# One mLSTM + ternary FFN layer: keys and queries stacked per head by DMA through memory, or by VectorE copies

## What is computed

```python
x = x + attn(layernorm(x))      # mLSTM with 8 heads, 32 query/key and 64 value channels a head
x = x + ffn(layernorm(x))       # 512 -> 2048 -> 512, ternary weights, exact gelu
# attn: q, k, v, o = x @ Wq.T, x @ Wk.T, x @ Wv.T, x @ Wog.T; i, f = soft_cap(x @ W.T + b)
#  per step: C = F*C + I*k v^T; n = F*n + I*k; h = (q.C)/max(|q.n|, exp(-m)); norm over the head;
#  y = (sigmoid(o) * norm(h) * gamma) @ Wout.T
```

## Time and profile before

| | |
|---|---|
| Median of 3 runs | 2092.59 us (2092.44 to 2092.97) |
| The profiled execution | 2091.54 us |
| Its span, first to last instruction | 2089.8 us |
| TensorE busy | 1901.8 us, 91% of the span |
| VectorE busy | 1565.6 us, 75% |
| ScalarE, GpSimd busy | 1032.0 and 568.6 us |
| Mean granted TensorE clock | 0.957 of full speed |

### The profile page before, as it was taken

One profiled execution on the slowest core, in us unless ns is written; L12 is line 12 of the kernel. 1 busy time (PEld: TensorE's weight loads), 2 busy tenths in 40 slices (PEclk: granted clock), 3 DMA queues, 4 the chain that ended last, 5 costly groups with the idle time before them and its releaser, 6 DMA issues.

```text
span 2089.8 us, 26265 instructions
## 1 busy us (share of the span) xinstructions
PE 1901.8 (91%) x9652; PEld 1001.9 (48%) x9652; DVE 1565.6 (75%) x2798; ACT 1032.0 (49%) x1711; POOL 568.6 (27%) x401
## 2 busy tenths in 40 slices
PE   4667898998989899898989989898998989899989
PEld 2253454644545464454536445453644545364544
DVE  3887869687786968778696877869687796957742
ACT  3654627465362645536264553626455362645523
POOL 1242142240324224032422403232140323214030
PEclk7868999999999999999999999999999999999999
DMA  6232314142231404224140322414042241404010
GB/s 247 89 106 78 82 46 124 26 99 46 83 88 46 124 21 104 46 73 97 46 124 21 104 46 63 107 46 124 21 104 46 53 117 41 109 21 109 1 46 21
DMA packets 233504, 156.62 MB, mean 75 GB/s; under 512 B 195088, under 2 KB 199312, under 8 KB 228256
## 3 DMA queue, kind: packets, MB, share of 16 engines
q1 hardware_dynamic: 231792, 151.79, 27.5%
q10 hardware_dynamic: 1584, 3.15, 0.4%
HBM read 90.48 MB, written 17.24 MB: 52 GB/s over the span
## 4 chain that ended last, share of the span: by engine, by line
PE 63%; DVE 25%; issue 6%; ACT 5%; DMA 1%; POOL 0%; SPq 0%; POOLq 0%; DVEq 0%; ACTq 0%
PE pf L1687 21%; PE pf L1673 16%; PE pa L1574 11%; DVE hoT L1194 10%; DVE gT L1194 5%; PE ph L1646 4%; PE pa L1565 4%; DVE cst L1187 2%; PE ph L1640 2%; DVE gT L1124 2%; PE ph L1612 1%; DVE cst L1185 1%; PE ps L1623 1%; PE pa L1556 1%; ACT L768 1%
## 5 line engine op out<-in xcount | busy, mean ns | idle before, releaser
L1687 PE MATMUL pf<-w2T,gT 128*128 128x512 f16 x2048 | 535.2, 379 | 0.0
L1673 PE MATMUL pf<-x2T,w1T 128*128 128x512 f16 x2048 | 496.5, 396 | 0.9 <-DVE x2T L1320 0.6
L1574 PE MATMUL pa<-wT,xT 128*128 128x512 f16 x1536 | 344.7, 381 | 5.8 <-ACT vaug L788 2.9
L1673 PEld LDWEIGHTS pf<-x2T,w1T 128*128 128x128 f16 x2048 | 204.1, 102 | 236.5 <-issue 38.6
L574 POOL TENSOR_TENSOR hinv<-hvar,half 128x8 f32<-128x8 f32 x64 | 105.1, 1643 | 749.1 <-DVE hvar L1279 749.1
L1687 PEld LDWEIGHTS pf<-w2T,gT 128*128 128x128 f16 x2048 | 224.3, 111 | 173.9
L856 ACT ACTIVATE g<-pf,b1c 128x512 f32<-128x512 f32 x256 | 175.4, 685 | 237.6 <-DVE gT L1328 133.5
L1328 DVE SCALAR_TENSOR_TENSOR gT<-g,wscale,gT 128x512 f16<-128x512 f32 x256 | 190.9, 751 | 127.7 <-ACT gT L859 127.2
L1194 DVE COPY hoT<-cst 32x1024 f16<-32x1024 f16 x256 | 253.8, 991 | 4.6
L1574 PEld LDWEIGHTS pa<-wT,xT 128*128 128x128 f16 x1536 | 145.8, 98 | 193.1 <-ACT sig L795 14.0
L560 POOL TENSOR_TENSOR dec<-dec,causal 128x1024 f32<-128x1024 f32 x64 | 159.9, 2527 | 252.5 <-DMA dec<-gate_r 252.5
(11 more groups left out here) (202 smaller groups left out, 2407.3 us busy)
## 6 DMA issues: line engine op xcount, KB each, us to landing
dec<-gate_r SPq DMA_DIRECT2D x32, 1024.0 KB, 6.3
xin<-L_attn_x SPq DMA_DIRECT2D x16, 1024.0 KB, 5.9
out<-x1b SPq DMA_DIRECT2D x64, 256.0 KB, 2.3
xres<-L_attn_x SPq DMA_DIRECT2D x16, 512.0 KB, 6.3
xres<-L_attn_x SPq DMA_DIRECT2D x32, 256.0 KB, 3.0
qw<-gate_w SPq DMA_DIRECT2D x128, 48.0 KB, 5.7
gT<-L_ffn_w SPq DMA_DIRECT2D x5, 1024.0 KB, 4.9
gT<-L_ffn_w ACTq DMA_DIRECT2D x3, 1024.0 KB, 5.5
```

Of the source, the lines that this page charges most:

```text
L1574: last = nc.tensor.matmul(bank, src[:, xs, k, :], wT[:, ws, k, col:col + D], start=(k == 0 and n == 0), stop=(k == KD - 1 and n == 2))
L1673: last = nc.tensor.matmul(bank, w1T[:, k, tok(f)], x2T[:, part, :, k, :], start=(k == 0 and part == HI), stop=(k == KD - 1 and part == LO))
L1687: last = nc.tensor.matmul(bank, gT[:, part, f, tok(t)], w2T[:, f, :], start=(f == 0 and part == HI), stop=(f == NF - 1 and part == LO), sk ...
```

## The change

`stack_heads` and its 32 copies are gone. VectorE splits the keys, then waits until the split is stored, splits the queries into the same buffer, and goes on. SyncE's queue stores each split (0.5 MB) to a new tensor in memory, `kq_halves`, waits for the landing, and reads it back in four transfers of 32 partitions (256 KB each) straight into the stacked layout. The keys' store is issued before the transposition to `x2T`, everything else behind it. The heads now lie in `kst` and `qst` in the order in which the scores take them. TensorE waits once, before `scores(b, 0)`, for all eight read-backs. The `qw` loads become four transfers of 96 KB in place of eight of 48 KB.

```diff
--- before.py
+++ after.py
@@ -61,7 +61,7 @@
 
 
 
-DVE_L, DVE_A = 3, 6 + 4 + 4 * 5 + 4 + 2
+DVE_L, DVE_A = 3, 6 + 2 + 4 * 5 + 4 + 2
 POOL_A = 4
 
 
@@ -109,6 +109,7 @@
 
     gate_r = nc.dram_tensor("gate_r", (B, NH, S), F32, kind="Internal").ap()
     gate_w = nc.dram_tensor("gate_w", (B, NH, LATE), F32, kind="Internal").ap()
+    kq_halves = nc.dram_tensor("kq_halves", (B, 2, P, 2, HG, S), F16, kind="Internal").ap()
 
     with ExitStack() as ctx:
         def sb(name, shape, dt=F32):
@@ -253,7 +254,8 @@
         masked = sem("masked")
         d_ok = sem("d_ok")
         qw_ok, fcol_ok = sem("qw_ok"), sem("fcol_ok")
-        k_ok, kq_ok = sem("k_ok"), sem("kq_ok")
+        kq_split, kq_stored = sem("kq_split"), sem("kq_stored")
+        k_stacked, q_stacked = sem("k_stacked"), sem("q_stacked")
         c_ok = sem("c_ok")
         sq_ok = sem("sq_ok")
         hvar_ok = sem("hvar_ok")
@@ -426,9 +428,28 @@
                                  .rearrange("p (h s) -> p h s", s=S)).then_inc(r_loaded[g], 16)
                 sp.wait_ge(w_stored, at(b, 16, 16))
                 for h in range(H4):
-                    for g in range(HG):
-                        sp.dma_start(qw[h * DQ:(h + 1) * DQ, g, :],
-                                     gate_w[b, g * H4 + h, :].partition_broadcast(DQ)).then_inc(w_loaded, 16)
+                    sp.dma_start(qw[h * DQ:(h + 1) * DQ, :, :],
+                                 gate_w[b, h::H4, :].partition_broadcast(DQ)).then_inc(w_loaded, 16)
+
+            def store_halves(b, use):
+
+                sp.wait_ge(kq_split, at(b, 2, use + 1))
+                sp.dma_start(kq_halves[b, use], kq_parts).then_inc(kq_stored, 16)
+
+            def stack_halves(b, use, stacked, order, done):
+
+                sp.wait_ge(kq_stored, at(b, 32, 16 * use + 16))
+                for r, part in enumerate(order):
+                    sp.dma_start(stacked[r * DQ:(r + 1) * DQ, :, :].rearrange("p (h g) s -> p h (g s)", h=H4),
+                                 kq_halves[b, use, :, part, :, :].rearrange("(h d) g s -> d h (g s)", d=DQ)
+                                 ).then_inc(done, 16)
+
+            def stack_keys(b):
+                stack_halves(b, 0, kst, (HI, HI, LO, LO), k_stacked)
+
+            def stack_queries(b):
+                store_halves(b, 1)
+                stack_halves(b, 1, qst(b), (HI, LO, HI, LO), q_stacked)
 
             def load_x(b):
 
@@ -482,6 +503,9 @@
             sp.wait_ge(pa_fill, x_index(0, KD - 1) + 1)
             load_x(1)
             gate_rows(0)
+            store_halves(0, 0)
+            stack_keys(0)
+            stack_queries(0)
 
             for n in range(4):
                 sp.wait_ge(s_tern, 4 * (n + 1))
@@ -492,11 +516,17 @@
             heads_out(0, None, lambda: sp.wait_ge(pa_fill, x_index(1, KD - 1) + 1), lambda: load_x(2))
             for b in range(1, B - 1):
                 gate_rows(b)
+                store_halves(b, 0)
                 transpose_x2(b - 1)
+                stack_keys(b)
+                stack_queries(b)
                 transpose_x(b + 1)
                 heads_out(b, b - 1)
             gate_rows(B - 1)
+            store_halves(B - 1, 0)
             transpose_x2(B - 2)
+            stack_keys(B - 1)
+            stack_queries(B - 1)
             residual(B - 1, RES_TILES[1])
             heads_out(B - 1, B - 2)
             for t in range(T):
@@ -1180,20 +1210,15 @@
 
             def split_parts(b, ch, use, whole):
 
+                if use == U_Q:
+                    dve.wait_ge(kq_stored, at(b, 32, 16))
+
                 for n in range(HG):
                     dve.wait_ge(pa_free[(use + n) % 2], pa_done(b, use + n))
                 nc.vector.tensor_scalar(kq_parts[:, HI, :, :], whole, split_scale[:, 0:1], None, ALU.mult).then_inc(dve_a, 1)
                 dve.wait_ge(dve_a, ch.next())
                 nc.vector.scalar_tensor_tensor(kq_parts[:, LO, :, :], whole, split_scale[:, 0:1], kq_parts[:, HI, :, :],
-                                               ALU.mult, ALU.subtract).then_inc(dve_a, 1)
-                dve.wait_ge(dve_a, ch.next())
-
-            def stack_heads(stacked, order, h, done):
-
-                for r, part in enumerate(order):
-                    last = nc.vector.tensor_copy(stacked[r * DQ:(r + 1) * DQ, h::H4, :],
-                                                 kq_parts[h * DQ:(h + 1) * DQ, part, :, :])
-                last.then_inc(done, 1)
+                                               ALU.mult, ALU.subtract).then_inc(kq_split, 1)
 
             def weigh_keys(b, chunks, src, free):
 
@@ -1213,11 +1238,13 @@
                 weigh_keys(b, (2,), pa[:, U_KLAST % 2, 0:QK], pa_free[U_KLAST % 2])
 
             def chunk_decay(b):
-                dve.wait_ge(w_loaded, at(b, 16 * NH, 16 * NH))
+                dve.wait_ge(w_loaded, at(b, 16 * H4, 16 * H4))
                 nc.vector.tensor_copy(fcol[:, :, :], qw[:, :, P - 1::P]).then_inc(fcol_ok, 1)
 
             def state(b, j):
 
+                if j == 0:
+                    dve.wait_ge(kq_stored, at(b, 32, 32))
                 dve.wait_ge(ph_fill, at(b, PH_USES, U_U + j + 1))
                 nc.vector.tensor_tensor(cst[:, j, :, :].rearrange("p a (h v) -> p a h v", v=VA),
                                         ph[:, :, 0:H4 * VA].rearrange("p a (h v) -> p a h v", v=VA),
@@ -1351,22 +1378,13 @@
                     norm_apply(b + 1)
                     weights_lo(*USES_O[2:4])
                 split_parts(b, ca, U_K, kT[:, :, :])
-                for h in range(H4):
-                    stack_heads(kst, (HI, HI, LO, LO), h, k_ok)
-                    if h == 1:
-                        keys_first(b)
-                        chunk_decay(b)
-
+                split_parts(b, ca, U_Q, qT[:, :, :])
+                keys_first(b)
+                chunk_decay(b)
                 if run_f and ahead:
                     tokens_lo(b + 1)
-                dve.wait_ge(k_ok, at(b, H4, H4))
-                split_parts(b, ca, U_Q, qT[:, :, :])
-                for h in range(H4):
-                    stack_heads(qst(b), (HI, LO, HI, LO), h, kq_ok)
-                    if not run_f and h == 1:
-                        thresholds()
-
-                dve.wait_ge(kq_ok, at(b, H4, H4))
+                if not run_f:
+                    thresholds()
                 def hidden(*fs):
                     if run_f:
                         for f in fs:
@@ -1617,10 +1635,11 @@
 
                 if not (isinstance(b, int) and b == 0 and n == 1):
                     pe.wait_ge(ps_free[n % 2], ps_done(b, n) - 1)
-                if n % HG == 0:
-                    pe.wait_ge(kq_ok, at(b, H4, n // HG + 1))
+                if n == 0:
+                    pe.wait_ge(k_stacked, at(b, 64, 64))
+                    pe.wait_ge(q_stacked, at(b, 64, 64))
                 for j in range(T):
-                    last = nc.tensor.matmul(ps[:, n % 2, tok(j)], kst[:, HEADS[n], tok(j)], qst(b)[:, HEADS[n], tok(j)],
+                    last = nc.tensor.matmul(ps[:, n % 2, tok(j)], kst[:, n, tok(j)], qst(b)[:, n, tok(j)],
                                             start=True, stop=True)
                 last.then_inc(ps_fill, 1)
```

## The result

Over 20 executions the changed kernel takes 2095.07 us (2092.56 to 2099.93), the kernel before 2091.2 beside them (2089.26 to 2093.65): a ratio of 1.0019, 95% interval 1.0012 to 1.0025. The change makes the kernel 3.9 us slower (0.2%), just under the 4.2 us that the prediction named as measurable, though the interval lies above 1; 12 us less were forecast. The profiled spans are 2092.7 and 2089.8 us. The time lies in the whole range that was stated (2030 to 2112), but outside the forecast's own (2057 to 2088), on its slower side.

A forecast was written before the change was run, and what follows sets the result against it. TensorE, busy 91%, was bound by waits at the scores, 6.0 us a block, set by VectorE's copies. 6 us from 15 blocks plus 6 from block 0 gave 12 less, 2080 us; range 2030 to 2112, the forecast's own 2057 to 2088.

The forecast's parts named there:

- T: Time the last read-back lands ahead of a block's scores; SyncE's chain of transfers was summed to 1087.4.
- the relation of the prediction: At the scores: a block wins 1087.8 - T, so 0.4 us, and loses if T is later than 1087.8.
- the factor of 15: Blocks 1 to 15 were each taken to win 0.4 us at the scores, 6 us together.
- The rate: Read-backs to 32 partitions: 240 GB/s taken, 4.4 us for 1.05 MB, plus 2.6 us for the rest of the transfer.
- Block 0: First block, no FFN: thresholds on VectorE come earlier without copies ahead; 6 us won, bounds 3 and 7.3.
- Covers: VectorE's work before T and `x2T`'s landing cost nothing; `outer` and `hidden(0)` don't wait; `transpose_x` delay is free.
- Rival A: Read-backs run at full rate, 347 GB/s: 3.2 us a block, 54 to 71 us less, 2022 to 2038; chance 0.22.
- Rival B: Slower: read-backs and the store between them, strictly one after another, take longer than the copies; up to 2115; chance 0.24.
- near bound: Read-backs at 212 GB/s: T 1.1 later, 1088.5, a loss of 0.7 a block, which block 0 about pays for.
- far end: Also the full 1.5 us at the transposition: T 1089.7, a loss of 1.9 a block, 22 us slower, 2115.
- Rival C: Nothing moves: the wait at the scores only changes its name, T within 0.3 us of 1088.2; chance 0.12.
- the figure of the Trainium skill: 32 partitions reach 8 of 16 ports, 189 GB/s at 1 MiB: read-backs 5.5 us each, some 20 us slower.

The follow-up runs named there:

- run 4: Changed kernel, blocks of 32 partitions kept, with `xin` and all behind it on SyncE's queue held until the queries' read-back landed: 2094.31 us, ratio 1.0017.
- runs 2 and 3: Changed kernel with each read-back going to every fourth partition: 2080.55 us; the same with `xin` also held until the queries' read-back landed: 2063.63 us.
- run 6: Changed kernel with the keys' read-back issued from ScalarE's queue instead of SyncE's: 2111.78 us, ratio 1.0094.
- run 9: Kernel before the change, with only `tokens_lo` moved behind the queries' 16 copies: 2125.58 us, ratio 1.0159.

## Why the prediction was wrong

The steps of the sum, against the block shown (its times plus 2.80):

| step | predicted | measured |
|---|---|---|
| keys' store issued | 1063.1 | 1063.0 |
| it lands, VectorE goes on | 1069.4 | 1069.1 |
| queries' split done | 1071.4 to 1076 | 1073.7 |
| transposition issued until | 1072.0 | 1072.3 |
| keys' read-back issued until | 1073.9 | 1074.4 |
| queries' store landed | 1080.4 | 1081.2 |
| queries' read-back landed, T | 1087.4 | 1088.3 |

This block waits 6.65 us, the mean of the fifteen is 6.9, so T is 1088.5 on average. By the relation of the prediction (a block wins 1087.8 - T) that is a loss of 0.7. The two timelines gave 0.52 for blocks 2 to 14, as the stretch from the first scores to `scores(b, 2)` takes 6.1 us there and not 6.3, and 2.8 for block 15. So the relation holds within 0.2 us a block; that the average over the blocks is 0.68 is luck.

**The step that failed is T, the landing of the last read-back: 1088.5 for the 1087.4 of the sum, 1.1 us late at the end of a chain 24 us long**, in terms that all err to the same side: 0.3 us on the transposition's issue (8.43 in this block), 0.2 on the keys' issue (2.00 for four), 0.3 on the stretch of read-back and store (6.8 from the end of the issue to the landing; 6.5 taken), 0.1 on the last read-back, and 0.2 between this block and the mean (the transposition's issue takes 9.19 in the block before it). None is large; but the forecast's win was 0.4 us, a difference of two chains of over 20 us each, and half of that error was enough to turn it. The sizes I could get within 1 us; the sign needed better than that, and 0.64 for faster was too much. A second, smaller fault is the factor of 15: the last block has no `tokens_lo` in the kernel before, and cost 2.8 us by itself.

**The rate** I took at 240 GB/s with 2.6 us around it: 7.0. In run 4 it was 217 (195 in its middle), 4.8 us, with 0.9 us ahead and 1.3 behind: 7.05 in all, as in the changed kernel. Two errors that cancel, by luck. The 212 GB/s of the `qw` row, which I set aside as too low for its small pieces, was the better guide.

**Block 0**: 6 forecast, 7.2 measured, near its upper bound of 7.3. Thresholds came at 84.97 (85.9 forecast), the scores at 97.97 (98 to 99).

**Covers**: as named. `x2T` landed in time; `outer` and `hidden(0)` did not wait; `tokens_lo` was done at 1073.8 of this block and the `xin` behind it cost no one. But the traffic of `xin`, and of what follows it, was not in the sum at all. It costs nothing with the slow blocks (run 4) and half of the gain with the spread (runs 2 and 3).

**Rival A**'s premise, no limit at 32 partitions, is wrong: with the limit taken away and `xin` held the kernel is 31.4 us faster, about 2 us a block, against 3.2 in the rival. **Rival B** at its near bound gave T 1088.5 and a loss of 0.7 a block, which block 0 about pays for. That came number for number, but not by its cause: it made each read-back 0.55 us longer, and the queries' took 7.1 us for the 7.0 of the forecast; the rest came from the other terms above. Its far end (2115 us) did not come. **Rival C**, nothing moves, with T within 0.3 us of 1088.2, describes the result as well: T was 1088.5 and the time moved by 3.9 us, less than the 4.2 named there. The T of 1089.6 that the figure of the Trainium skill gave was 1.1 too late: it put 2.6 us on top of 5.5 for each read-back, 8.1, where 7.05 were measured (4.8 for the data and 2.2 around them).

## What to carry to other kernels

Before pricing an edit as a whole, ask of each piece how long its consumer can wait: here half of the transfers (the keys') had 18 us of cover, and the kernel with them alone is 5% faster (block 0 and the new order included); the other half, on the path, gave all of it back. Ask too how much of a piece its consumer needs to start: behind the queries' split, a store of 0.5 MB and a read-back of 1 MB took 14.6 us, with the queue's other work between them, and all of it had to land; 16 copies took 8.5, and the first scores needed four of them. When the forecast is a small difference of two long chains, say the size with confidence and the sign without. Look also at the first and the last turn of a loop before you multiply by the number of turns. And when lifting a limit gives a third of what it should, look at once for what was issued right behind it.

## What was not expected of the hardware

- A transfer to partitions four apart instead of 32 neighbours ran at about 300 GB/s (with nothing issued behind it) instead of 195, at the price of a longer issue (0.63 us each for 0.43 to 0.50).
- A transposing transfer and plain read-backs at the same time stretch each other: 18.2 us to landing for 10.8, and 9.4 for 5.1 (run 6). Why is open; nothing here separates the engines from memory.
- What the lower clock costs depends on where the idle time lies: in front of work that something else holds up anyway it is partly free; in front of work on the path, 8 matmuls cost 1.7 us more (run 9).
- VectorE's second pass of the split took 3.26 us beside GpSimd's mask and 1.28 elsewhere. The Trainium skill (SBUF — State Buffer, "Who interferes with whom") says that a VectorE instruction with two SBUF inputs contends with a GpSimd instruction that reads SBUF; this row agrees. The first pass, with one tensor as input, took 1.34 us beside the mask too, for 0.75 elsewhere.
- Left open: why even the spread read-back, with nothing issued behind it, shows a DMA share of 0.82 to 0.85 and under 300 GB/s in its second half; and the chain with both the keys' read-back spread and the queries by copies, which was not tried.
